# A gated mixer and a mixture of experts on one core: expert weights split once by ACT and an adding DMA, 128-row blocks, rows added into two DRAM accumulators

## The reference, cut to what matters

```python
x = L0_attn_x                                   # 4 x 2048 x 512, 8192 tokens
mod = (silu(c) @ wmod).reshape(4, 6, 1, 512)    # sa, ca, ga, sb, cb, gb
h = layernorm(x) * (1 + ca) + sa
x = x + ga * mixer(h)        # rms norm, in projection, 4-tap convolution, state space in chunks of 128, gate, out projection
h = layernorm(x) * (1 + cb) + sb
scores = sigmoid(h @ w_router)                  # 64 experts in 8 groups
topk = top 8 of (scores + b_router) in the best 4 groups
w = 2.5 * scores[topk] / sum(scores[topk])
y = sum over the 8 chosen e of w_e * (silu(h @ gate_e) * (h @ up_e)) @ down_e    # 512 x 256, 512 x 256, 256 x 512
shared = (silu(h @ ws_gate) * (h @ ws_up)) @ ws_down
x = x + gb * (y + shared)
...
```

## Time and profile before

| | |
|---|---|
| median of 3 runs | 7290.77 us (7288.45 to 7290.84) |
| profiled execution, its own time | 7291.05 us |
| its span, first to last instruction | 7289.1 us |
| PE busy | 6353.5 us (87%) |
| DVE busy | 5795.8 us (80%) |
| ACT busy | 3685.3 us (51%) |
| POOL busy | 3110.3 us (43%) |
| mean granted clock of PE | 0.932 of full speed |

### The profile page before, as it was taken

One profiled execution on the slowest core, in us unless ns is written; L12 is line 12 of the kernel. 1 busy time (PEld: TensorE's weight loads), 2 busy tenths in 40 slices (PEclk: granted clock), 3 DMA queues, 4 the chain that ended last, 5 costly groups with the idle time before them and its releaser, 6 DMA issues. The chain is left out here.

```text
span 7289.1 us, 126851 instructions
## 1 busy us (share of the span) xinstructions
PE 6353.5 (87%) x30107; PEld 4618.2 (63%) x30107; DVE 5795.8 (80%) x13553; ACT 3685.3 (51%) x7314; POOL 3110.3 (43%) x3483
## 2 busy tenths in 40 slices
PE   4888888888888888886999999999999999987665
PEld 2555555555555555554888888888888888863322
DVE  3888888888888888885888888888888888867666
ACT  2444444444444444443666666666666666652121
POOL 1555555555555555553222222222222222227776
PEclk8999999999999999997999999999999999998787
DMA  3000000000000000002444444444433444347777
GB/s 120 18 18 13 18 16 15 18 13 18 18 13 18 15 16 18 13 15 80 143 142 161 139 155 141 135 141 136 148 126 124 162 157 135 107 146 249 244 246 222
DMA packets 270703, 698.78 MB, mean 96 GB/s; under 512 B 53780, under 2 KB 53908, under 8 KB 261300
## 3 DMA queue, kind: packets, MB, share of 16 engines
q0 software_dynamic: 108544, 302.36, 13.4%
q1 hardware_dynamic: 69816, 226.96, 8.9%
q10 hardware_dynamic: 92160, 167.81, 7.1%
HBM read 476.38 MB, written 220.58 MB: 96 GB/s over the span
## 5 line engine op out<-in xcount | busy, mean ns | idle before, releaser
L1220 POOL DMA_INDIRECT xg_e<-h_dram,place x640 | 628.2, 982 | 2310.5 <-PE bank L1238 2270.8
L1325 DVE TENSOR_TENSOR w_lo<-w_exp,w_hi 128x768 fp32r<-128x768 f32 x1280 | 1216.1, 950 | 8.4 <-ACT w_hi L1293 8.4
L1182 PE MATMUL bank<-w_hi,x_hi 128*128 128x512 f32 x2560 | 1066.8, 417 | 0.4 <-DVE w_lo L1325 0.4
L1293 ACT CAST w_hi<-w_exp 128x768 fp32r x1280 | 1005.5, 833 | 53.7 <-SPq L1197 53.3
L1182 PE MATMUL bank<-w_hi,x_lo 128*128 128x512 f32 x2560 | 1015.6, 397 | 0.0
L1182 PE MATMUL bank<-w_lo,x_hi 128*128 128x512 f32 x2560 | 1015.0, 396 | 0.0
L862 DVE SCALAR_TENSOR_TENSOR acc<-raw,conv_w,acc 128x128 f32<-128x128 f32 x1920 | 814.5, 496 | 25.3 <-ACT acc L594 19.2
L1308 ACT COPY y_e<-bank 128x512 f32<-128x512 f32 x640 | 375.7, 587 | 725.4 <-PE bank L1182 725.4
L696 PE MATMUL bank<-xn_t,w_in 128*128 128x128 f32 x5120 | 590.5, 277 | 70.0 <-ACT xn_t L573 70.0
L696 PEld LDWEIGHTS bank<-xn_t,w_in 128*128 128x128 f32 x5120 | 578.3, 192 | 85.4 <-ACT xn_t L573 85.4
L533 POOL DMA_INDIRECT list_dram<-tok_id,pos x512 | 559.2, 1092 | 159.2 <-issue 154.4
(11 more groups left out here) (254 smaller groups left out, 12920.4 us busy)
## 6 DMA issues: line engine op xcount, KB each, us to landing
y_dram<-y_e ACTq DMA_DIRECT2D x640, 256.0 KB, 2.4
w_exp<-in_w_experts_dram SPq DMA_DIRECT2D x64, 1536.0 KB, 7.1
xin<-in_x_dram SPq DMA_DIRECT2D x64, 256.0 KB, 2.6
x_dram<-x SPq DMA_DIRECT2D x64, 256.0 KB, 2.0
h_dram<-h SPq DMA_DIRECT2D x64, 256.0 KB, 2.0
h_c<-h_dram SPq DMA_DIRECT2D x64, 256.0 KB, 5.0
x_c<-x_dram SPq DMA_DIRECT2D x64, 256.0 KB, 3.6
out_dram<-o_c SPq DMA_DIRECT2D x64, 256.0 KB, 4.5
```

The lines of the kernel that those rows point to most:

```text
L1182: last = nc.tensor.matmul(acc, a, b, start=(i == 0), stop=(i == len(terms) - 1))
L1220: pool.indirect_dma_start(xg[:, q, :], None, h2_dram, bass.IndirectOffsetOnAxis(ap=place[:, q:q + 1], axis=0)).then_inc(g_in[q], 16)
L1293: nc.scalar.copy(w_hi[:, (q // 2 + 1) % 2, part], raw).then_inc(S["split_hi"], 1)
L1325: nc.vector.tensor_tensor(w_lo[:, pair, part], raw, w_hi[:, pair, part].bitcast(FP32), ALU.subtract).then_inc(S["split_lo"], 1)
```

## The change

Its parts:

- **Weights.** The mixer's steps also split the experts' weights, one set (the shared expert first, then the 64) per step `ws` = s + 1, in two parts of 1536 columns. SP loads a part into `w_raw`. ACT rounds it to `w_hi_m`, which SP stores to `hi_dram`, and then writes the negative of the rounded part over `w_raw`. SP has also copied the set from DRAM to `lo_dram`; POOL adds `w_raw` to it by a DMA. So `lo_dram` holds weight minus rounded weight. In `experts()` SP loads both; nothing is split there.
- **Blocks** of 128 rows instead of pairs: 65536 / 128 + 64 = 576.
- **Routing** without one-hot tiles: `match_replace` marks the eight best with a large number, a comparison makes `picked`, another the dense weights `wd`, which are stored as 64 more columns of h2 (`ROW` = 576). The positions come from a key and `max`.
- **Rows.** ACT loads the token numbers of a block straight from `list_dram`; POOL gathers h2 rows with them; ACT scales the result by the expert's column; POOL adds the rows by an indirect DMA to one of two accumulators in DRAM, used in turn.
- **combine()** loads both accumulators. POOL adds them, DVE adds the shared expert, now in three split products like the others, POOL applies the gate and adds x1.
- Setup also clears the accumulators by ACT's queue (2 x 17 MB), and keeps `mod` of two batches instead of four, loading the others later.

```diff
+        def split_hi(act, j, i):
+            act.wait_ge(w_ld[i], 16 * (j + 1))
+            nc.scalar.copy(w_hi[:, i, :], w_raw[:, i, :]).then_inc(S["w_hi"], 1)
+            act.wait_ge(S["w_hi"], PARTS * j + i + 1)
+            nc.scalar.activation(w_raw[:, i, :].bitcast(FP32R), w_raw[:, i, :], ACT.Copy, scale=-1.0).then_inc(S["w_neg"], 1)
+        def split_lo(pool, j, i):
+            pool.wait_ge(lo_cp, 16 * (j + 1))
+            wait_apart(pool, S["w_neg"], PARTS * j + i + 1, passed)
+            pool.dma_start(part_of(set_of(lo_dram, j), i), w_raw[:, i, :], accum_op=ALU.add).then_inc(lo_st[i], 16)
...
             def _(sp):
-                def step(e, f, c, t, q, p):
+                def step(e, f, c, t, q, p, ws):
+                    if ws is not None:
+                        for i in range(PARTS):
+                            sp.wait_ge(S["w_hi"], PARTS * ws + i + 1)
+                            sp.dma_start(part_of(set_of(hi_dram, ws), i), w_hi[:, i, :].bitcast(FP32)).then_inc(hi_st[i], 16)
...
                     if c is not None:
                         sp.wait_ge(S["x1_done"], c + 1)
                         sp.dma_start(rows_of(x1_dram, c), x1[:, p, :]).then_inc(x1_st[p], 16)
+                    if ws is not None and not (isinstance(ws, int) and ws == NSET - 1):
+                        for i in range(PARTS):
+                            sp.wait_ge(hi_st[i], 16 * (ws + 1))
+                            sp.wait_ge(lo_st[i], 16 * (ws + 1))
+                            sp.dma_start(w_raw[:, i, :], part_of(set_of(w_experts_d, ws), i)).then_inc(w_ld[i], 16)
+                        sp.dma_start(set_of(lo_dram, ws + 1), set_of(w_experts_d, ws)).then_inc(lo_cp, 16)
...
             def _(act):
+                def step(e, f, c, t, q, p, ws):
+                    if ws is not None:
+                        split_hi(act, ws, 0)
                     if c is not None:
                         act.wait_ge(S["dt_done"], c + 1)
...
-                        route.mark(nc.vector.max_index(out=eidx[:], in_max=emax[:], in_values=ms[:]))
+                        route.mark(nc.vector.match_replace(out=msr[:], in_to_replace=emax[:], in_values=ms[:], imm_value=BIG))
...
+                        ts(picked[:], msr[:], BIG, None, ALU.is_equal).then_inc(S["picked_done"], 1)
+                        route.mark(stt(out=wd[:], in0=msr[:], scalar=BIG, in1=sc[:], op0=ALU.is_equal, op1=ALU.mult))
-                        route.mark(tt(oh[:], iota_e[:].unsqueeze(1).to_broadcast([P, TOPK, EXPERTS]),
-                                      eidf[:].unsqueeze(2).to_broadcast([P, TOPK, EXPERTS]), ALU.is_equal))
-                        nc.vector.tensor_reduce(picked[:], oh[:].rearrange("p k e -> p e k"), AX.X, ALU.add).then_inc(S["picked_done"], 1)
...
@@ experts(), the program of POOL @@
+                def step(b, q):
+                    ahead, old = b + 3, b - 2
+                        pool.indirect_dma_start(xg[:, r, :], None, h2_dram,
+                                                bass.IndirectOffsetOnAxis(ap=ids[:, r:r + 1], axis=0)).then_inc(g_in[r], 16)
+                    if valid(old):
+                        pool.wait_ge(S["y_sb"], old + 1)
+                        if not (isinstance(old, int) and old < NACC):
+                            added(pool, old - NACC, r - NACC)
+                        pool.indirect_dma_start(acc_dram[r % NACC], bass.IndirectOffsetOnAxis(ap=ids[:, r:r + 1], axis=0),
+                                                y[:, r % YSLOTS, :], None, compute_op=ALU.add).then_inc(y_st[r % YSLOTS], 16)
@@ experts(), the program of PE @@
+                        e = pe.value_load(entry(tab_e, b), min_val=0, max_val=EXPERTS - 1)
+                        at_b = e % WSLOTS * WPE
+                        pe.wait_ge(S["w_ready"], e + 1)
```

More of the change, by code:

```diff
@@ L1112, in tables @@
-    return dict(idx=idx, tab_e=tab_e, tab_col=tab_col, tab_end=tab_end, base=base, rows=out_rows)
-def experts(nc, top, sem, tile, bank, half, env, tab):
-    ident, h2_dram, y_dram, w_d = env["ident"], env["h2_dram"], env["y_dram"], env["w_experts"]
-    SLOTS, WSLOTS = 4, 3
+                for j in range(2):
+                    cols = slice(j * HB, (j + 1) * HB)
+                    nc.tensor.matmul(half(4 + j)[:, 0:HB], ones[0:E - 1, :], ge[0:E - 1, cols], start=True, stop=True)
+                    last = nc.tensor.matmul(half(6 + j)[:, 0:HB], blk_col[0:E - 1, 0:1].to_broadcast([E - 1, P]),
+                                            ge[0:E - 1, cols], start=True, stop=True)
@@ L1152, in entry, with steps @@
             return t[0:1, i:i + 1] if isinstance(i, int) else t[0:1, bass.ds(i, 1)]
-        def steps(eng, step):
-            for b in range(-2, SLOTS):
+        def steps(eng, step, first=-1):
+            for b in range(first, SLOTS):
                 step(b, b % SLOTS)
@@ L1229, in _ @@
+                steps(pool, step, first=-3)
+                for q in range(YSLOTS):
+                    pool.wait_ge(y_st[q], 16 * NBLK // YSLOTS)
             @block.tensor
@@ L1271, in step @@
                 def step(b, q):
-                    ahead, nxt, prev, old = b + 2, b + 1, b - 1, b - 2
+                    ahead, nxt, prev = b + 4, b + 1, b - 1
+                    if valid(ahead):
+                        r = (q + 4) % SLOTS
+                        row = act.value_load(entry(tab_row, ahead), min_val=0, max_val=PADS)
+                        if not (isinstance(ahead, int) and ahead < SLOTS):
+                            added(act, ahead - SLOTS, r)
+                        act.dma_start(ids[:, r:r + 1], list_dram[bass.ds(row, P), :]).then_inc(l_in[r], 16)
                     if valid(nxt):
@@ L1347, in step @@
                     if valid(b):
-                        found.wait()
-                        found.mark(nc.vector.tensor_reduce(first[:], pick[:], AX.X, ALU.add))
-                    if valid(ahead):
-                        split(0)
-                    if valid(b):
-                        found.wait()
-                        found.end()
-                        nc.vector.tensor_tensor(out_rows[:, at], first[:], top_r[:, at], ALU.add)
                         r = q % 2
```

619 lines of the change are left out of this document (292 added, 327 removed).

## The result

| | median (runs) |
|---|---|
| before | 7289.6 us (7287.4 to 7290.8, 4 runs) |
| after | 7593.4 us (7572.6 to 7596.4, 4 runs) |
| ratio | 1.041, 95% interval 1.040 to 1.042 |

A forecast was written before the change was run, and what follows sets the result against it. It took PE to bind the expert stage, a dependency loop the mixer, and gathers to hold up the last stage. 7291 + 18 + 605 - 10 - 253 - 429 = 7222, stated as 7220 us, range 7030 to 7520.

The forecast's parts named there:

- Setup, +18: Setup: clearing 34 MB on ACT's queue shares the DMA engines with the loads, mostly running under the mixer; +18 us.
- The two bounds, 0 and 89: Setup: clearing adds at best nothing, at worst all of its about 89 us of all 16 engines.
- Mixer, +605: Mixer: ACT's first split waits for the late w_raw load, delaying `lm`; period 59.6 instead of 50.0 us, +605 us.
- the load, 4.4 us forecast: Mixer: the 768 KB w_raw load, taken between measured landings of 256 KB and 1536 KB; 4.4 us.
- The prediction's other estimate of this load, 3.8 us: Mixer: w_raw load by the DMA page, 2.0 us plus bytes over 436 GB/s; 3.8 us, sum 38 us lower.
- The rival of a larger wait: Mixer: load takes 7.1 us and PE runs at 1.2 GHz after idling; 252 us more, 7474 us; chance 0.16.
- Tables, -10: Between mixer and experts: the list's load and its 33 transposes go; -10 us.
- Experts, -253: Expert stage: 576 blocks of 4.96 us instead of 640 of 4.86, PE still binding; -253 us.
- about 0.7, which still leaves room: Expert stage: DMA share with 1.2 MB a block, some 235 GB/s; about 0.7, not binding.
- The rival of PE's issue: Expert stage: both register reads per block show 0.40 us, block 5.66 us; 403 more, 7625 us; chance 0.10.
- The adds bind: Expert stage: one adding DMA at a time per accumulator; landing 11 us, block 6.15 us, 7907 us; chance 0.09.
- Combine, -429: Last stage: gathers and their sums go, PE binds at 4.96 us a chunk; -429 us.

The follow-up runs named there:

- e1: Changed kernel with SP's w_raw loads and the copy into lo_dram issued ahead of the store of h2, not behind that of x; 6815 us, ratio 0.935.
- e12: Changed kernel with ACT's first split and POOL's first add moved to the middle of the step, SP's order kept; 6941 us, ratio 0.952.
- e11: Changed kernel without the experts' weight loads after the first three, but for 64 of 3072 columns; 7323 us, ratio 1.004.
- e9: Changed kernel with DVE copying token numbers for the add, numbers loaded seven and gathers issued five blocks ahead, loops still eight; 7378 us, ratio 1.012.
- e8: Changed kernel with rows written over each other in the accumulators instead of added; 7426 us, ratio 1.019.
- e2: Changed kernel with sixteen slots for token numbers instead of eight, ACT's and POOL's loops sixteen blocks long; 7618 us, ratio 1.045.
- e4: Changed kernel with accumulators cleared by SP in 256 KB pieces, two per mixer step, instead of in the setup; 7529 us, ratio 1.033.

## Why the prediction was wrong, point by point

- **Setup, +18, measured +50.** A term mis-sized, and half of it a wait that the forecast did not have. It counted only what the loads lose by sharing the DMA engines, whose share is 0.99 through 148 us. But the second clearing transfer also held ACT at its issue for 60.9 us, so that PE began 26 us after its weights had landed; the later loads of the setup add the rest. The two transfers land after 69 and 134 us (101.8 is the mean of these), and neither runs under the mixer, where the forecast had placed most of it. The two bounds, 0 and 89, held.
- **Mixer, +605, measured +689.** The mechanism and its place were right, its size nearly, and e1 and e12 show them by two different moves. Mis-sized: the load, 4.4 us forecast; the first half, on which ACT waits, lands after 5.0 us in the median and the second after 6.5, as two loads of 768 KB and a copy of 1.5 MB are issued within 1.7 us. In e1, where the halves start 10.5 us apart, they take 6.4 and 4.4, so what runs beside a load decides and not its size alone. (The prediction's other estimate of this load, 3.8 us, lies further off.) And the eight products of L763, 3.69 us before, took 6.23 behind 12.3 us in which PE had no work. The sum also has a slip: its distances come from a period of 50.6 us, but the 59.6 were set against the mean of 50.0; set against 50.6 it would have been +567, further off. The rival of a larger wait (4.0 us a period) was a third right: the period grew by 10.9 us, 1.3 more than the 9.6, just where that rival was to decide.
- **Tables, -10, measured +7.** The 33 transposes are gone, but the expert stage now begins with token numbers loaded beside 6 MB of weights: POOL's first gather starts at 4139.9 us, 12 us after SP's first weight load.
- **Experts, -253, measured -10.** This is the step that failed: "about 0.7, which still leaves room". The share is 0.74 at 5.38 us a block, so the mean was about right; the room is not there when it is wanted. 3 MB of weights come at once and fill all engines for more than 10 us, once per expert. Small transfers then land late (adds after 11.3 us instead of 4.9), and the forecast had looked at none of the waits that then end late: ACT's for the add of four blocks before, ahead of `x_hi` and `h_hi`, and POOL's for the token numbers, ahead of a gather that had 3 blocks. e11 (no burst) takes 259 us off the stage, e9 (no such waits, deeper) 206 and e8 (no adding) 155; e2 shows, its own loop stall set aside, that to remove the add's wait alone is not enough. The Trainium skill (DMA: Bandwidth & Descriptors, Rules for kernel authors) says that transfers of all issuing engines run on the same 16 DMA engines and interleave; the trace agrees in that SP's loads delay POOL's adds and ACT's loads.
- **The other parts of the block were nearly right.** PE's two reads per block cost nothing that can be seen in seven blocks of eight: the median is 4.83 us against 4.86. At the turn of the loop PE does stand on issue, 35 us in 79 places and about 48 us by the length of the blocks, where 58 were forecast (0.1 us in each of 576 blocks). The rival of PE's issue (0.10) is out. By the Trainium skill (DMA: Bandwidth & Descriptors, Latency and other measured facts), with its floor of about 600 ns per such load, the two would be an estimated 1.2 us; here they measure 0.30 us each, 0.6 together, and the measurement decides (L1304, 576 reads: 296 ns the shortest, 303 the median, 1018 the longest).
- **The adds bind** (0.09) was the nearest rival in kind, and wrong in mechanism. It priced the turn of an accumulator, decided at a landing of 8.4 us, and asked for POOL waiting: POOL waited 37 us for adds, ACT 231. A median landing of 4.9 us does not decide; 11 to 14 us in a burst do.
- **Combine, -429, measured -431.** 4.81 us a chunk against 4.96.

## What to carry to other kernels

A mean DMA share below 1 says little of a stage in which megabytes come at once: ask how long a small transfer takes inside the burst, and which engine waits for it with work of others queued behind. A wait for a transfer belongs behind the engine's urgent work, or far enough back that even the slowest landing has passed; three transfers of SP, issued ahead of two stores instead of behind them, were worth 778 us here. And issue a large transfer from an engine that has nothing urgent behind it. When a loop is unrolled further for more buffers, look at the instruction queue.

## What was not expected of the hardware

- Unrolling ACT's and POOL's loops from eight to sixteen blocks brought instruction packets from 3 to 44 in 700 us, and about 4 us of standing still at one block in sixteen (4.5 in the turn shown), in a stage with a DMA share of 0.74.
- Writing rows by an indirect transfer without the add, in place of with it, shortened the other transfers too: the weights' second load from 13.8 to 11.5 us.
- Issuing a clearing transfer of 17 MB behind another of that size held ACT for 60.9 us; the first took it 0.6 us to issue, and two pieces of 256 KB on the same queue in e4 took 0.5 us each.
